# Weight loads issued ahead of the stage barriers in an eight-core attention and FFN kernel

## The reference

```
x = x + layernorm(attn(layernorm(x), z_q, b_q, z_k, b_k, w_v, b_v))
x = x + layernorm(ffn(layernorm(x), W_r, W_k, W_v, mu_r, mu_k))

attn: Q, K = poincare_fully_connected(x, z, b)   # x @ z, then arcsinh, sinh, a norm
      V = x @ w_v.T + b_v
      softmax(Q K^T / 8) V, 16 heads of 64, sequence 2048
ffn:  xr, xk = mixes of x and x shifted by one position
      out = sigmoid(xr @ W_r.T) * (relu(xk @ W_k.T)**2 @ W_v.T)
```

## Time and profile before

| | us |
|---|---|
| median of 3 runs | 3400.09 (3394.73 to 3418.83) |
| the profiled execution | 3398.45 |
| its span, slowest core (core 0) | 3396.7 |
| spans of the eight cores | 3383.0 to 3396.7 |
| mean granted TensorE clock, eight cores | 0.800 to 0.805 of full speed |

### The profile page before, as it was taken

How to read it: one execution, slowest core, us unless ns; L and a number is a source line. 1 busy time by engine, 2 the same in 40 slices (tenths; PEclk the granted TensorE clock), 3 DMA queues, 4 the chain that set the end, 5 groups by cost and what they waited for, 6 DMA issues and landing times.

```text
span 3396.7 us, 27929 instructions; the slowest of 8 cores (3383.0 to 3396.7 us)
## 1 busy us (share of the span) xinstructions
PE 1853.9 (55%) x7360; PEld 575.7 (17%) x7360; DVE 1452.8 (43%) x2455; ACT 1684.8 (50%) x1721; POOL 162.6 (5%) x256
## 2 busy tenths in 40 slices
PE   0364352277687687780506454414776877778504
PEld 0121120011121121120202121101111212212101
DVE  2255554111544625536425555440126264364363
ACT  0253655277747647651102653654776575664501
POOL 0001001100000000000000011010000000000000
PEclk9986676588898898895757776667888988989857
DMA  5513011622404313311162122017223232241211
GB/s 80 109 50 75 19 31 38 122 74 64 94 19 106 87 34 95 79 27 52 22 126 59 45 58 50 19 39 135 69 62 87 41 92 67 50 122 29 64 25 38
DMA packets 325786, 217.10 MB, mean 64 GB/s; under 512 B 276224, under 2 KB 284544, under 8 KB 325632
## 3 DMA queue, kind: packets, MB, share of 16 engines
q1 hardware_dynamic: 287488, 109.87, 14.8%
q0 software_dynamic: 38144, 105.45, 12.9%
HBM read 169.03 MB, written 42.21 MB: 62 GB/s over the span
## 4 chain that ended last, share of the span: by engine, by line
ACT 30%; DVE 25%; PE 24%; DMA 9%; issue 7%; SPq 2%; DVEq 1%; ACTq 1%; POOL 0%; POOLq 0%
ACT pool L1102 16%; PE psc L946 3%; PE psc L682 3%; DVE pool L870 3%; PE psc L926 3%; PE psc L645 3%; DMA pool<-x 3%; PE p_attA L1046 2%; DVE dump L371 2%; DVE dump L368 2%; DMA pool<-s_vaug 2%; PE psc L1077 2%; ACT pool L537 2%; ACT pool L540 2%; PE p_attB L1054 2%
## 5 line engine op out<-in xcount | busy, mean ns | idle before, releaser
L1102 ACT ACTIVATE pool<-psc 128x1024 bf16<-128x1024 f32 x1024 | 1048.9, 1024 | 571.3 <-PE psc L1084 493.2
L1046 PE MATMUL p_attA<-pool 128*65 128x512 bf16 x1024 | 433.5, 423 | 392.1 <-ACT pool L1102 206.5
L1077 PE MATMUL psc<-pool 64*128 64x512 bf16 x1024 | 422.6, 423 | 91.4 <-DMA pool<-s_vaug 91.4
L1054 PE MATMUL p_attB<-pool 128*65 128x512 bf16 x1024 | 431.8, 422 | 0.0
L1084 PE MATMUL psc<-pool 64*128 64x512 bf16 x1024 | 423.1, 423 | 0.0
L1107 DVE CAST pool<-p_attA 1x512 bf16<-1x512 f32 x64 | 43.8, 685 | 822.4 <-PE p_attB L1054 801.8
L682 PE MATMUL psc<-w_sb,pool 128*128 128x512 bf16 x512 | 143.0, 445 | 288.1 <-DVE pool L697 288.1
L905 PE MATMUL psc<-pool,w_sb 128*128 128x512 bf16 x512 | 134.6, 422 | 246.0 <-DVE smc L893 238.0
L1046 PEld LDWEIGHTS p_attA<-pool 128*65 128x65 bf16 x1024 | 114.9, 112 | 719.6 <-issue 719.6
L461 PE MATMUL psc<-dump,ones_bf 128*128 128x512 bf16 x64 | 34.4, 561 | 284.5 <-DVE dump L455 284.5
L1077 PEld LDWEIGHTS psc<-pool 64*128 64x128 bf16 x1024 | 91.3, 94 | 558.6 <-issue 558.6
(11 more groups left out here) (128 smaller groups left out, 2397.7 us busy)
## 6 DMA issues: line engine op xcount, KB each, us to landing
pool<-s_vaug SPq DMA_DIRECT2D x64, 520.0 KB, 4.8
pool<-s_kfm SPq DMA_DIRECT2D x64, 512.0 KB, 3.4
pool<-x POOLq DMA_DIRECT2D x8, 2048.0 KB, 9.4
pool<-x POOLq DMA_DIRECT2D x32, 512.0 KB, 3.8
out<-pool POOLq DMA_DIRECT2D x32, 512.0 KB, 2.9
s_vaug<-pool POOLq DMA_DIRECT2D x32, 260.0 KB, 2.3
s_qfm<-pool POOLq DMA_DIRECT2D x32, 256.0 KB, 4.4
s_kfm<-pool POOLq DMA_DIRECT2D x32, 256.0 KB, 4.6
```

The lines of the kernel that those rows point to most:

```text
L1046: T(lambda t, c=c, po=po, vof=vof: t.matmul(p_attA[0:65, :], vsl[:, vof:vof + 65], PT[:, po:po + 512], start=(c == 0), stop=(c == 15), ski ...
L1054: tk = T(lambda t, c=c, po=po, vof=vof: t.matmul(p_attB[0:65, :], vsl[:, vof + 65:vof + 130], PT[:, po + 512:po + 1024], start=(c == 0), s ...
L1077: T(lambda t, kof=kof, qof=qof, reg=reg: t.matmul(psc[:, reg:reg + 512], Ksl[0:64, kof:kof + 128], Qsl[0:64, qof:qof + QB], start=True, st ...
L1102: lambda s, reg=reg, po=po: s.activation(PT[:, po:po + 1024], psc[:, reg:reg + 1024], AF.Exp, scale=0.125),
```

## The change

The three places at which a weight set is changed after the start are rewritten.

- At the end of each projection stage the FFN's set is issued ahead of `emit_tails`, with a wait for the last projection matmul. The barrier now comes after these loads in the program, and so waits for them too.
- At the end of the first attention stage zq and zk are issued between `emit_ffn1` and `emit_ffn2`, with a wait for the last FFN matmul. wvT is issued after `emit_ffn3`, and POOL first waits until zk has landed. The barrier comes after all three and waits for them.

The first load of the kernel and the end of the second sequence stay as they are. No computation is changed, and the bytes that are moved are the same.

```diff
@@ -743,10 +743,10 @@
             pc["xnf_free"][par] = p.last["t"]
             bnd_p = {"qb": qb, "base": base, "hev": hev_toks,
                      "Aq": Aq2[par], "Ak": Ak2[par], "par": par}
+        tk_wset = load_wset(["wrT", "wkT", "wfT"], p.last["t"])
         emit_tails(bnd_p)
         bnd_p = None
         p.barrier()
-        tk_wset = load_wset(["wrT", "wkT", "wfT"], None)
@@ -1163,12 +1163,17 @@
         emit_bndC(pend_b)
         emit_bndD(pend_b)
         emit_ffn1(pend_b)
+        if s_i + 1 < NSEQ:
+            tk_w01 = load_wset(["zq", "zk"], p.last["t"])
         emit_ffn2(pend_b)
         emit_ffn3(pend_b)
+        if s_i + 1 < NSEQ:
+            tk_wset = G(lambda g: g.dma_start(
+                out=r3(w_sb[:, 2 * NCH * D:3 * NCH * D], D),
+                in_=w_in["wvT"].rearrange("(c p) d -> p c d", p=128)),
+                waits=[tk_w01], inc=16, sem="g_w")
         pend_b = None
         p.barrier()
-        if s_i + 1 < NSEQ:
-            tk_wset = load_wset(["zq", "zk", "wvT"], None)
```

## The result

| | before | changed |
|---|---|---|
| median of 10 runs each, us | 3401.04 (3394.73 to 3418.83) | 3349.34 (3343.39 to 3365.77) |
| ratio, 95% interval | | 0.9847 (0.9826 to 0.9868) |
| spans of the eight cores in the profiled run, us | 3383.0 to 3396.7 | 3333.0 to 3347.2 |
| mean granted clock, eight cores | 0.800 to 0.805 | 0.806 to 0.810 |

The changed kernel is 1.5% faster, 52 us. Forecast were 3353.6 us; the range was 3328 to 3374. Timed twice more, it gave 0.9853 (0.9831 to 0.9874) and 0.9859 (0.9829 to 0.9888). In the profile of the second timing one die stood at a lower clock than the other; it is left out of what follows.

The account below looks back on a forecast made before the run. No engine's busy sum was taken to set the time; waits for loads at attention starts and the change of sequence were read singly. From 3398.45 us, A took 43.5 and B 1.3, giving 3353.6 us, range 3328 to 3374.

Parts of the forecast that it names:

- A: End of both projection stages: issuing the FFN's set ahead of the last tails saves 43.5 us.
- B: Change of sequence: issuing zq and zk ahead of the last transposes, wvT behind the last store, saves 1.3 us.
- undisturbed head pair: Starts of attention: with loads alone, V lands 6.8 us after K's issue, plus 0.1 to the first matmul.
- two first head pairs: Starts of both attention stages: TensorE starts earlier, saving 21.3 us at the first and 15.2 at the second.
- stall of the second pair: Second attention start: the second head pair is late by 8.78 us, of which 7.0 is saved; nothing at the first start.
- 1.82: Switch of head pairs in attention: 1.82 us of wait stays, since PV waits for the evacuation anyway.
- 1398 of the transposes' packets: Change of sequence: 1398 of 4224 transpose packets are gone before zq's first packets; 2826 then take turns with the weights.
- its bounds: Limits of B at the change of sequence: 22.6 us saved if transposes are not slowed, −2.0 if they get nothing until 1724.1.
- The transposes did not escape: Rival at the change of sequence: turns granted more freely to transposes, B gives 22.6 us, time 3332.4; chance 0.13.
- The weights were not held up by DVE: Rival beside the tails: busy DVE delays the weights 22 us, A falls to 21.5, time 3375.6; chance 0.07.
- The clock gave nothing back: Rival in attention: lower clock more often after shorter rests, 0.23 us more per matmul, time 3374; chance 0.10.
- The slower case: Rival at the new barrier: weights land 76.7 us after issue, gain lost; at 100 us, time is 3445; chance 0.04.

Follow-up runs that it names:

- e4: Changed kernel with only zq issued ahead of the last transposes, zk and wvT behind the last store; 3344.5 us (one run).
- e3: Changed kernel with zq and zk issued after the last block's transposes have landed; ratio to the kernel before 0.984, on repeat 0.9815.
- e6: Changed kernel with the FFN's set issued about 40 us later, ahead of the last step of the tails; 3386.2 us (one run).
- e1: Kernel before with only the FFN's set moved ahead of the last tails (A alone); ratio to the kernel before 0.9876.
- e2: Changed kernel with the FFN's set back behind the barrier (B alone); ratio to the kernel before 1.0003.
- e5: Changed kernel with projection weights issued after the transposes, last stores and first x load on SP's queue, barrier skipping the weights' semaphore; ratio to before 0.9799.
- e7: e5 with each projection weight issued once its slot is free, zq and zk during the FFN, wvT after the transposes; ratio to before 0.9736.

## Why the prediction was right

**In sum.** On the mean of the eight cores 49.5 us were won, where 44.8 were forecast. A gave 46.5 (said 43.5) and B 0.6 (said 1.3); 3.2 came from the second projection stage, for which the prediction had no term. The mechanisms were right. Inside A and inside B terms were off and partly made up for each other.

**Part A.** The issue came at the end of the projections, the three loads took 44.1 us (said 44.0), 10.9 us were to spare (said 10.9), and V to K stayed at 76. The undisturbed head pair took 7.5 and 7.2 us on the mean (said 6.9). The waits for V loads, 91.4 us on core 0, are 48.9 in two on the changed kernel's slowest core (said about 48):

```profile
PE psc L1077 <- DMA pool<-s_vaug: 48.9, 2, 25.7
```

The two first head pairs gave 35.3 us (said 36.5). The stall of the second pair is the term that was too small. I read it off core 0, where it was 0.9 us at the first stage and hid under the evacuation. On core 6 it kept TensorE idle from 681 to 689 (window 681:685 us of the kernel before, no matmul):

```profile
681.00:685.00 4.00, 0.00 (x0) 0.00 (x0) 2.70 (x4) 0.00 (x0) 0.53 (x1) 0.76 1.12 203
```

Over the eight cores this stall runs from 0.85 to 11.1 us, on the mean 6.2 at the first stage and 6.0 at the second, and in the changed kernel no core has it. So it is not true that each core loses the same waits. Less 1.82 on each core, as in the prediction, it is worth 8.7 us in the two stages, by estimate, where 7.0 were forecast. From the first matmul to the end the two attention stages gave 3.3 and 7.9, together 11.2. What the other 2.5 are is not shown; with the stall still there, B alone already has 1028.3 and 1073.5 us for these two stages, so some of it may be scatter.

**Part B.** The sums start 24.9 us later (said 25.4), with equal counts on both queues, and F to X changed by 0.6 us (said 1.3). That the sum came so close is in part luck, since two terms of it were off. The prediction let 1398 of the transposes' packets go ahead of the weights. They did not: by 1679, 4.6 us after the last FFN matmul, 2 had gone (window 1674:1679), and on every core their first packet came after the weights' first. So more were left when the weights were through (window 1704:1707, the transposes' queue):

```profile
q0 software_dynamic: 54, 0.11, 33.1%
q1 hardware_dynamic: 2, 0.00, 0.1%
...
q1 hardware_dynamic: 2233, 0.55, 114.1%
```

Against that, the turns were faster, 79 per us where 71.8 were taken from the V loads. The 21.2 us expected of e4 rest on the same two terms. Why the transposes started late is open.

That the value lies where the prediction put it between its bounds is shown: e4 and e3 have the hold proportional to the weight packets, and none without them. One load alone landed in 15.7 us instead of the 18.1 used. The Trainium skill, DMA: Bandwidth & Descriptors (Queues, rings and completion order), has each engine switch between its queues at packet boundaries; 1737 against 1737 packets agree with it.

**The rivals.** The transposes did not escape. The weights were not held up by DVE: 44.1 us beside the tails, 44.0 behind the barrier. The warning of the Trainium skill, SBUF — State Buffer (SBUF: two separate sides), that a DMA issued from GpSimd waits while DVE holds their shared port, does not show at this kernel's tails. The clock gave nothing back: the attention stages became shorter, and the mean clock rose a little. The slower case needs loads of 77 us, and no run had them; e6 shows what late weights cost, by the stores of Q behind them.

**What was not foreseen.** 3.2 us in the second projection stage. There, 150 to 180 us behind X, TensorE's clock stands longer at its upper level (2.4 GHz, the lower being 1.2). Same work, windows of before (core 0), then changed (core 2); PE's busy time is the first number behind the length, the clock the last but two:

```profile
1929.00:1959.00 30.00, 9.80 (x24) 3.16 (x24) 16.94 (x29) 7.34 (x13) 1.08 (x2) 0.61 0.28 54
...
1907.00:1937.00 30.00, 7.16 (x24) 2.49 (x24) 18.51 (x31) 7.59 (x15) 1.08 (x2) 0.67 0.28 54
```

24 matmuls took 9.80 us of busy time before and 7.16 after. These are single cores; on the mean of the eight the granted clock of this window is 0.63 before and 0.67 after, and 0.65 against 0.71 in the next 30 us. The stage is 434.6 to 435.6 us in the changed kernel, its repeat, e3, e4 and e6, and 437.3 to 438.5 in before, e1, e2, e5 and e7. So it repeats, and comes neither with A alone nor with B alone. That the clock makes the 3.2 us is argued from this, not shown by a run of its own, and why it rises earlier in the one group is open.

## What to carry to other kernels

A bulk load moved early is free only if nothing that is waited for shares the DMA engines or its queue with it meanwhile. In part A that held by 10.9 us; in e6 stores stood behind the loads on one queue, and the gain was gone. Transfers of small packets suffer most. Count the packets of what the load will run beside: in turns, each small packet waits for a large one, whatever the bytes. And issue a weight when its own slot comes free, not when the whole set does. From the last FFN matmul to x it took 86 us with the loads behind the barrier, 85 with two of them ahead of the transposes, 70 with these two behind the transposes, and 44 with each at its slot and the stores and x on another queue.

## What the hardware showed beyond expectation

- Turns are by packet, and a turn lasts about as long as both packets. 256-byte packets beside 2 KB ones went at 79 of each per us (1737 in 22 us), where alone the small ones go at over 600 (2826 in 4.45 us) and the large ones at 82. x's 4 KB packets beside the same weights went at 40 per us, and x took 19.7 us where it takes 9.3 alone.
- Each load of 1024 packets delayed the transposes by 12.5 us, for one load and for two, to within 0.1 us.
- TensorE's clock in a sparse stretch settled in one of two patterns that repeat from run to run of a kernel (0.63 or 0.67 of full speed over 30 us, mean of eight cores). They go with a stage that is 2 to 3 us longer or shorter.
